# A decoder layer on one core: a second bank for the first batch, early unit-matrix products, the division as one product, and the place of some weight splits

## What is computed

```python
x = x + attn(layernorm(x))
# attn, per batch:
qkv = x @ qkv_w.T + qkv_b
q, k = rope(q), rope(k)
logits = q @ k.T * SM_SCALE          # masked: k > q, or k <= q - 128
m = max(logits)
e = exp(logits - m)
w = e / (sum(e) + exp(sink - m))     # the division
out = (w @ v) @ out_w.T + out_b
```

## Time and profile before

| | us |
|---|---|
| median of 3 runs | 2067.29 (2065.62 to 2067.77) |
| the profiled execution | 2068.88 |
| its span, first to last instruction | 2067.10 |
| TensorE busy | 1963.5 (95%) |
| VectorE busy | 1609.0 (78%) |
| ScalarE busy | 928.8 (45%) |
| GpSimd busy | 781.9 (38%) |
| issue of the identity's load on SyncE | at 1.73 |

### The profile page before, as it was taken

How to read it: one execution, slowest core, us unless ns; L and a number is a source line. 1 busy time by engine, 2 the same in 40 slices (tenths; PEclk the granted TensorE clock), 3 DMA queues, 4 the chain that set the end, 5 groups by cost and what they waited for, 6 DMA issues and landing times.

```text
span 2067.1 us, 45595 instructions
## 1 busy us (share of the span) xinstructions
PE 1963.5 (95%) x15488; PEld 1606.9 (78%) x15488; DVE 1609.0 (78%) x5780; ACT 928.8 (45%) x3481; POOL 781.9 (38%) x883
## 2 busy tenths in 40 slices
PE   5899999999999988989999999999998999999899
PEld 5688888888888867778888888888886677777687
DVE  4777877777778776667777777777777899999887
ACT  3555555555455544545555554554553222222233
POOL 3444434333333332322333323323322455555454
PEclk8999999999999999999999999999999999999999
DMA  5246211111111211111211111111104533232343
GB/s 174 75 103 144 73 52 63 52 52 70 55 52 62 85 61 58 48 50 64 80 54 52 53 52 52 53 63 52 52 33 170 164 101 89 86 87 87 98 143 123
DMA packets 71545, 162.25 MB, mean 78 GB/s; under 512 B 6657, under 2 KB 15233, under 8 KB 71185
## 3 DMA queue, kind: packets, MB, share of 16 engines
q1 hardware_dynamic: 62864, 142.54, 20.6%
q0 software_dynamic: 3840, 8.39, 2.2%
q10 hardware_dynamic: 4608, 8.39, 1.1%
HBM read 108.96 MB, written 50.41 MB: 77 GB/s over the span
## 4 chain that ended last, share of the span: by engine, by line
PE 69%; DVE 20%; ACT 5%; issue 4%; POOL 1%; DVEq 0%; DMA 0%; ACTq 0%; POOLq 0%
PE banks L504 17%; PE banks L564 14%; PE banks L519 9%; PE banks L1103 8%; PE banks L543 7%; PE banks L1309 4%; PE banks L497 4%; PE banks L529 4%; ACT pr L636 3%; DVE pr L849 3%; DVE m L825 2%; DVE terms L1135 2%; DVE banks L1149 2%; DVE pr L866 1%; DVE banks L1145 1%
## 5 line engine op out<-in xcount | busy, mean ns | idle before, releaser
L636 ACT ACTIVATE pr<-pr,mx 128x128 f32<-128x128 f32 x1024 | 399.0, 391 | 439.1 <-DVE mx L849 439.1
L710 POOL TENSOR_TENSOR m<-m,rope_sb 128x512 f32<-128x512 f32 x160 | 206.7, 1292 | 522.0 <-ACT m L623 522.0
L504 PE MATMUL banks<-xTh,wh 128*128 128x256 f32 x1280 | 378.9, 296 | 7.4 <-DVE xTl L809 4.0
L504 PE MATMUL banks<-xTl,wh 128*128 128x256 f32 x1280 | 365.4, 285 | 0.0
L504 PE MATMUL banks<-xTh,wl 128*128 128x256 f32 x1280 | 365.0, 285 | 0.0
L1103 PE MATMUL banks<-kv,tap 128*128 128x288 f32 x1280 | 323.9, 410 | 12.7 <-DVE res L1159 10.9
L1103 PEld LDWEIGHTS banks<-kv,tap 128*128 128x128 f32 x1280 | 238.1, 190 | 98.1 <-issue 36.5
L504 PEld LDWEIGHTS banks<-xTh,wh 128*128 128x128 f32 x1280 | 248.5, 194 | 11.3 <-issue 5.7
L504 PEld LDWEIGHTS banks<-xTl,wh 128*128 128x128 f32 x1280 | 249.0, 195 | 0.0
L858 DVE TENSOR_TENSOR den<-ac,es 128x4 f32<-128x4 f32 x256 | 52.2, 204 | 252.7 <-ACT es L639 252.7
L504 PEld LDWEIGHTS banks<-xTh,wl 128*128 128x128 f32 x1280 | 248.5, 194 | 0.0
(11 more groups left out here) (108 smaller groups left out, 3849.4 us busy)
## 6 DMA issues: line engine op xcount, KB each, us to landing
tap<-padded_taps SPq DMA_DIRECT2D x64, 256.0 KB, 3.3
kk<-in_ctxt SPq DMA_DIRECT2D x64, 192.0 KB, 3.4
x_in<-in_x SPq DMA_DIRECT2D x16, 512.0 KB, 4.0
xt_split<-xTh SPq DMA_DIRECT2D x16, 512.0 KB, 2.7
xt_split<-xTl SPq DMA_DIRECT2D x16, 512.0 KB, 3.8
xb<-in_x SPq DMA_DIRECT2D x16, 512.0 KB, 4.6
factors<-in_factors POOLq DMA_DIRECT2D x8, 1024.0 KB, 8.5
x_part_rows<-x SPq DMA_DIRECT2D x16, 512.0 KB, 3.0
```

What stands on the lines that cost most here:

```text
L504: last = pe.matmul(wP[:, h * T:(h + 1) * T], w[:, n, c, h * P:(h + 1) * P], a[:, s, c, :], start=(c == 0 and i == 0), stop=(c == KD - 1 an ...
L636: act.activation(pr[:, s, a, cols], pr[:, s, a, cols], ACT.Exp, bias=mx[:, s, i:i + 1], scale=-1.0, accum_out=ac[:, s, i:i + 1])
L710: pool.tensor_tensor(m2[:, s], m2[:, s], rope_sb[:, 1 if i == 0 else 0, 1:3], ALU.mult).then_inc(sin_ready, 1)
```

## The change

It has four parts. The identity matrix `id_sb` is loaded by ScalarE's queue, as its first instruction, and no longer as SyncE's third. TensorE makes 12 transposes of the identity into bank `pP` before the first transposes of x. For the first batch (`unit_bank`: first body, steps 0 to 3), the second half of x is transposed into `oP`, and units 1, 2, 3 and 5 are made in `oP`, while unit 0 and V stay in `wP`; what each waits for changes with it, as do the readers' banks, and the first body's output projection waits for the turn of unit 5. The division becomes one product with the reciprocals broadcast over 128 columns. And outside the first body, `split_low` moves from the end of its slot to the beginning of the next one (`split_last`).

```diff
+    def unit_bank(y, p, n):
+        return oP if y.first and p < 4 and n not in (0, V_UNIT) else wP
+    def split_last(y, p, j):
+        k = 2 * p + j - 1
+        if y.first or y.number == 1 and k < 0:
+            return []
+        if k < 0:
+            return split_now(Body(y.m - 1, 0, y.number - 1), 7, 1)
+        return split_now(y, k // 2, k % 2)
...
-        sp.dma_start(id_sb[:], ident).then_inc(id_in, 16)
...
-        def x_transposes(v, t):
+        def x_transposes(v, t, bank=wP):
             pe.wait_ge(xn_ready, 2 * v + t + 1)
-            wait(pe, m_ready, 0 if isinstance(v, int) and v == 0 else (QM + 1) * (v - 1) + 2 + t)
-            wait(pe, xt_lo, 2 * v + t)
+            if v == 1:
+                pe.wait_ge(m_ready, 1)
+            elif v > 1:
+                pe.wait_ge(m_ready, (QM + 1) * (v - 1) + 2 + t)
+            if v > 0:
+                wait(pe, xt_lo, 2 * v + t)
...
         # unit_free
+            if v == 0:
+                wait(pe, m_ready, (0, 0, 2, 3, 1, 4)[n])
+                if n == V_UNIT:
+                    pe.wait_ge(xt_lo, 4)
+                return
+            if v == 1 and n == 0:
+                pe.wait_ge(v_ready, 1)
...
         # out_projection
+            if y.first:
+                pe.wait_ge(m_ready, QM + 1)
...
-        for t in range(NT):
-            x_transposes(0, t)
+        for n in range(12):
+            pe.transpose(pP[:, 0:P], id_sb[:], id_sb[:])
+        x_transposes(0, 0)
+        x_transposes(0, 1, oP)
...
+        act.dma_start(id_sb[:], ident).then_inc(id_in, 16)
         split_high(0, 0)
         x_high(0, 0, 0, 0)
-        x_high(0, 0, 1, 0)
+        x_high(0, 0, 1, 0, oP)
...
         # divide
-            for a in range(2):
-                for t in range(NT):
-                    cols = slice(t * P, (t + 1) * P)
-                    i = 2 * a + t
-                    last = dve.tensor_scalar(pr[:, s, a, cols], pr[:, s, a, cols], rden[:, s, i:i + 1], None, ALU.mult)
-            last.then_inc(pn_ready, 1)
+            quarters = pr[:, s].rearrange("p a (t k) -> p (a t) k", t=NT)
+            dve.tensor_tensor(quarters, quarters, rden[:, s].unsqueeze(2).broadcast_to([P, 2 * NT, P]), ALU.mult).then_inc(pn_ready, 1)
...
         # VectorE's body
                 for j in range(2):
+                    for i, n in split_last(y, p, j):
+                        split_low(i, n)
                     if residual_tile(y, p, j) is not None:
...
-                    for i, n in split_now(y, p, j):
-                        if not (y.first and n >= NU):
-                            split_low(i, n)
+                    if y.first:
+                        for i, n in split_now(y, p, j):
+                            if n < NU:
+                                split_low(i, n)
```

More of the change, by code:

```diff
@@ L444, in tensor @@
         pe.wait_ge(id_in, 16)
[L446 removed]
+        def x_transposes(v, t, bank=wP):
             pe.wait_ge(xn_ready, 2 * v + t + 1)
[L449 to L450 removed]
+            if v == 1:
[4 more added lines that the diff above has]
+                wait(pe, xt_lo, 2 * v + t)
             for c in range(KD):
[L452 removed]
+                last = pe.transpose(bank[:, c * P:(c + 1) * P], xn[:, t, c * P:(c + 1) * P], id_sb[:])
             last.then_inc(xt_done, 1)
@@ L491, in unit @@
             unit_free(y, p, n)
+            bank = unit_bank(y, p, n)
             steps = [(wh, xTh), (wh, xTl), (wl, xTh)]
@@ L496, in unit @@
                         for i, (w, a) in enumerate(steps):
-                            last = pe.matmul(wP[:, t * T:(t + 1) * T], a[:, s, c, t * P:(t + 1) * P], w[:, n, c, :],
+                            last = pe.matmul(bank[:, t * T:(t + 1) * T], a[:, s, c, t * P:(t + 1) * P], w[:, n, c, :],
                                              start=(c == 0 and i == 0), stop=(c == KD - 1 and i == 2))
@@ L503, in unit @@
                         for i, (w, a) in enumerate(steps):
-                            last = pe.matmul(wP[:, h * T:(h + 1) * T], w[:, n, c, h * P:(h + 1) * P], a[:, s, c, :],
+                            last = pe.matmul(bank[:, h * T:(h + 1) * T], w[:, n, c, h * P:(h + 1) * P], a[:, s, c, :],
                                              start=(c == 0 and i == 0), stop=(c == KD - 1 and i == 2))
@@ L614, in x_high, with bent @@
             wait(act, xt_saved[s], 32 * saves)
-            act.copy(xTh[:, s, :, t * P:(t + 1) * P], wP[:].rearrange("p (c n) -> p c n", c=KD)).then_inc(xt_hi, 1)
-        def bent(y, p, i):
+            act.copy(xTh[:, s, :, t * P:(t + 1) * P], bank[:].rearrange("p (c n) -> p c n", c=KD)).then_inc(xt_hi, 1)
+        def bent(y, p, i, bank):
             v = y.window(p)
@@ L622, in bent @@
             for half in range(2):
-                last = act.activation(m2[:, s, 1 - half], wP[:, half * T:(half + 1) * T], ACT.Identity,
+                last = act.activation(m2[:, s, 1 - half], bank[:, half * T:(half + 1) * T], ACT.Identity,
                                       bias=bqk_sb[:, y.sweep, i, half:half + 1])
@@ L824, in turned @@
             for half in range(2):
-                last = dve.scalar_tensor_tensor(m1[:, s, half], wP[:, half * T:(half + 1) * T], bias[:, half:half + 1],
+                last = dve.scalar_tensor_tensor(m1[:, s, half], bank[:, half * T:(half + 1) * T], bias[:, half:half + 1],
                                                 tab[:, 0], ALU.add, ALU.mult)
```

14 lines of the change are left out of this document (7 added, 7 removed).

## The result

The changed kernel took 2049.32 us in the median of 4 runs (2049.04 to 2049.52), the kernel before 2067.53 beside it (2065.62 to 2068.94). The ratio is 0.9912, with an interval of 0.9898 to 0.9927: faster by 18.2 us, where 13.1 were forecast. The profiled execution took 2049.21, its span 2047.4 against 2067.1 before.

The account below looks back on a forecast made before the run. TensorE's queue was taken to bound the kernel, so VectorE savings pay only where TensorE idles, while time won at the start carries through. Start 7.7 plus division 5.4 made 13.1 us: 2067.29 to 2054.2, range 2050 to 2061.

Parts of the forecast that it names:

- Start: Chain up to the first mask minimum of batch 0: at 34.2 against 41.90, 7.7 us gained, bounds 6.0 to 9.9.
- The second bank: Start: x's second four transposes no longer wait for the first bank, so unit 0 starts 1.3 us earlier, at 12.3.
- Identity beside x: Start: loading the identity on ScalarE's queue shares the first engines' time with x, 0.2 us lost, bounds 0 to 0.5.
- Unit products: Start: twelve transposes of the identity lie in time when TensorE has nothing else; in the sum they do nothing.
- Rival (a): Start: unit products raise the clock, unit 0 runs at the high clock, 2.2 us more gained, 2052.0; chance 0.15.
- Division: VectorE's division as one product, 0.2 us saved each where it is on the chain: 5.4 us in all.
- The terms for 44 to 184: Division: six on the chain between 44 and 100 give 1.2 us; four waits from 100 to 183.6 give 0.8.
- the term of 2.5 us for the change of sweeps: Division there: ten TensorE waits give 2.0 us, one caught division 0.5 more, the rest of its 1.08 hidden under TensorE's queue.
- Low parts of the weights: VectorE's low parts move to the next slot's beginning: order of instructions is the same, 0 us, waits for casts stay.
- (b): GpSimd's work or the load of x's batch 2 becomes last, half of the start's 7.7 lost: 2058.1; chance 0.15.
- (c): Division: the product is no faster than four scalings, only the 7.7 remains: 2059.6; chance 0.10.
- (d): Product over 0.88 us holds up the ring on some 25 divisions; at 1.5 us, 2075; steady stretches hide it; chance 0.03.

Follow-up runs that it names:

- changed_again: The changed kernel run once more with nothing edited: 2051.63 us (2047.84 to 2052.59 in four runs).
- four_scalings: The changed kernel with the division put back to four scalings of 128 columns: 2061.20 us.
- sync_no_units: The changed kernel with the identity loaded third on SyncE and without the 12 unit products: 2050.62 us.
- product_only: The kernel before with only the division replaced by one product: 2059.59 us.
- identity_on_sync: The changed kernel with the identity loaded third on SyncE again, the 12 unit products kept: 2045.43 us.
- more_unit_products: The changed kernel with 18 unit products instead of 12, identity on ScalarE's queue, and the weights' low parts moved behind the turn: 2041.86 us.
- both_finds: The changed kernel with the identity third on SyncE, 12 unit products, and the weights' low parts moved behind the turn: 2043.13 us.
- four_products: The changed kernel with the division cut into four products of 128 columns: 2061.67 us.
- product_twice: The changed kernel with a second, equal division product into a tile that nothing reads: 2120.45 us.

## Where the prediction was right, and the step that failed

- **Start: right.** 7.7 us forecast; 8.4 at copy 0 in the profile after, 8.7 in changed_again, 8.2 in four_scalings, whose median shows 7.1. (The 11.34 of the working should be 11.32; nothing hangs on it.) The steps came as put: identity landing 3.7 us after its issue, second transposes before 10, unit 0 at 11.6 (12.3 forecast), units 0 and 1 back to back, unit 2 at 24.7 (24.9) at the low clock, first mask minimum at 33.5 (34.2). The second bank, 1.3 forecast, measured 1.1 to 2.1.
- **Identity beside x: not seen.** 0.2 us was set for it. x landed 3.9 to 4.5 us after its issue, with the identity beside it or not (3.97 and 4.44 without, in sync_no_units and product_only; 3.99 in after), so any price is smaller than that spread.
- **Unit products: nothing, as in the sum, but not for the reason given.** Rival (a), that they raise the clock, did not happen in this change. Its mechanism is real: it came in the three kernels whose products ran up to the transposes without a pause. Its price of 2.2 us is close to the 1.9 by which unit 0 got shorter. The Trainium skill (TensorE: Matmul & The Clock Gate, Part 4: PE-mode transpose) says that transposes do not count as a busy engine; identity_on_sync, more_unit_products and both_finds contradict it, since TensorE had done nothing but transposes when their clock rose (9.8, 8.8 and 9.6 us); so the prediction leaned on a rule that is wrong here.
- **Division: right in kind, too small in size.** The terms for 44 to 184 held: 1.2 and 0.8 forecast, 0.9 to 1.2 and 0.9 measured. The steady stretch gave 0.7 to 1.2 for 0.3, the drain and second sweep 0.9 to 1.1 for 0.6.
- **The step that failed is the term of 2.5 us for the change of sweeps.** Alone, in product_only, it is 4.9. It was counted as ten waits of 0.2 and half a microsecond of one caught division, with the rest of its 1.08 called hidden under TensorE's own queue. The ten waits held, as ten steps of 0.18. Time lost in long divisions was not hidden: 1.45 us came at once at copy 141, behind the third of the long divisions, which the sum had at its plain 0.2, and 0.4 at copy 125. Behind the one that the sum did count (756.70), product_only, with a low clock at 744.1, gained nothing, and the kernel after, with none there, 1.3 us. The 1.42 us at copy 143 are the low clock's. Before and four_products have three divisions of 2 us, four_scalings one; with a single product there are one or two of 1.4 to 1.8 us, or none. But `den` is caught as well, six to seven times, which neither the sum nor the rivals had, and how much of the 4.9 us is owed to fewer collisions in all, and how much to where the clock fell, one profile of each kernel can't tell apart.
- **The whole gained 6.8 us there in the profile after, and 5.2 in changed_again.** In after, 1.3 us come at copy 121, behind the division at 756.70, and 1.5 at copy 125, behind the one at 788.78. A third jump, 1.4 at copy 127, is a low clock at 794 us that before had and after hadn't.
- **Low parts of the weights: right.** Same order, same time; moving them past something gives 4 to 6 us.
- **Rivals.** (b) nothing of the start was handed back as far as copy 117; in four_scalings the change of sweeps took 0.9 us more, with 6.8 us more of low clock. (c) the product is faster, by 0.18 us. (d) did not occur, but its sentence that the steady stretches would hide a slower product is wrong: product_twice lost 29.5 us in them. Its two products take 1.29 us together and it is 51.5 us over the kernel before beside it (2068.94), where (d) had 2075 for a product of 1.5 us.
- **The rest.** Medians of 8.7 and 7.1 for the two halves make 15.8, while the whole gave 18.2 in after and 16.9 in changed_again, against the kernel before beside each. At the change of sweeps the profiled execution was 1.6 us luckier than changed_again, more than the 0.7 us by which the range was missed; the median of changed_again, 2051.63, lies inside it. The failed term doesn't depend on that luck: it stands at 4.9 in product_only. What decides where the low clock falls from one execution to the next is open. So is how much of identity_on_sync's 3.9 us at that place (195.84 against 199.69) is owed to the earlier start and how much to chance; its own 31.70 at copy 0 explains only 1.5 to 2 us of its lead.

## What to carry to other kernels

Several short VectorE instructions in a row cost more than one that does their work: 0.18 us each time here, and they stand open to GpSimd for longer. Where a GpSimd instruction holds one, a microsecond is at stake; count such places in the trace, for the small neighbours too, and don't take them for hidden unless the waiting engine's own row shows slack. What each pays in the end varied here between nothing and 1.5 us. Compare the same slot in several kernels before you name a cause: a spell of low clock costs as much as a held instruction. Products that shall warm TensorE paid only where they ran right up to the real work; with a pause behind them they gave nothing to unit 0. And "this stretch has no idle time" says what a faster step is worth there, not what a slower one costs.

## What the runs showed of the hardware, unexpected

- Transposes of the identity and of x, with no other product before them, raised TensorE's clock (unit 0 in 3.13 us instead of 4.94, in three kernels in which they ran without a pause). The rise came under a granted clock of 1.00, which the record does not tell from the slow pace. In a fourth the clock rose too (8.8 us) and was gone again after 1.67 us of waiting.
- Four products of 128 columns with two SBUF inputs cost 898 ns, four scalings 875, one product of 512 columns 692: what is per instruction outweighs the kind.
- A scaling, product or addition of VectorE with its inputs in SBUF that begins under a GpSimd instruction of 1.3 us, or with it, is held by up to 1.2 us (a scaling of 0.28 took 1.42, an addition of 4 columns 1.23 instead of 0.15), and one that met two of them in a row by 2.7 (`den` at 159.44 in the kernel after, 2.87 us); one that began 0.17 to 0.24 us ahead gets through, and GpSimd's takes 0.3 to 0.4 us longer. The turns, which have an input from PSUM, weren't held (0.48 us in 304 cases).
